# First convolution of images 2 to 7 on 64x32 tiles of TensorE, with a DMA-made copy for the shifted corner

## Chip, cores, metric

One Trainium2 chip, one of its cores. The metric is the device time of one execution in microseconds (us). A time below is counted from the start of the profiled execution's span unless it is a duration.

## What is computed

The input x is 8 images of 32 channels, 128 x 128, float32. Cut to what matters, the reference is:

```
def _gn(v):        # groups of 2 channels, mean and variance over a group and the whole image
    ...
def _L0_conv_ref(x, weight, bias):     # x and weight quantised with one scale per tensor
    s = max(|x|);  q = clip(round(x * 127 / s), -127, 127)
    out = conv3x3(qx, qw, padding=1) * (sx * sw / 127**2) + bias
def _L1_conv_ref(image, weight1, weight2):
    kern = einsum(weight, PSI)                       # 3x3 kernels
    h = leaky(instnorm(conv3x3(image, kern1)))
    return leaky(instnorm(conv3x3(h, kern2)))
x = x + _L0_conv_ref(_gn(x), weight, bias)           # "x1" below
x = x + _L1_conv_ref(_gn(x), weight1, weight2)
```

So each image passes three 3x3 convolutions of 32 to 32 channels. Here they are called conv0 (quantised, fp16 operands), conv1 and conv2 (float32).

## The kernel before

**Layout.** An image of 128 x 128 is cut by the parity of column and row into four planes of 64 x 64, and the 128 partitions hold (column parity px, row parity py, channel). So a plane has 32 partitions, and partitions 0 to 63 are the even columns, 64 to 127 the odd ones. `xs` holds all 8 images. A tile with a border of zeros (66 x 66) feeds a convolution: `qpad` (fp16, the quantised image) conv0, `apad` conv1, `hpad` conv2.

**Tiles of TensorE.** A 3x3 tap of a full-size image becomes a tap among the four planes. The weights are gathered into 32-column blocks by how far the window is shifted: `own` (none), `side` (one column), `vert` (one row), `corn` (both). conv0 reads all 128 partitions for each plane of the output: a tile is 128 rows by 32 columns, 4 of them stand side by side, and each half unit (one PSUM bank, 512 columns) needs 4 parts of 4 matmuls. conv1 and conv2 work with 64x32 tiles, 8 side by side: 4 matmuls read 64 partitions for bank `hp` and 4 the other 64 partitions for the other bank; after that the halves change places. They need no corner: the missing taps are inside the 64 partitions.

**Units.** An image is 4 units of 2 PSUM banks. The results go through `ring`, 3 slots of 2 banks. A unit's first matmul waits until the unit 3 places before it was taken out of PSUM (`wait_slot`). conv0's units are taken by VectorE (`x1_unit`: times `dequant`, plus x, into `xs`), those of conv1 and conv2 by ScalarE (`take`), after VectorE's statistics of them (`conv_stats`).

**Order.** Every engine's order is written out by hand. After a head (loading, group statistics, the global maximum, images 0 and 1 of conv0) come six periods t = 0 to 5, and TensorE does in each conv1 of image t, conv0 of image t + 2 and conv2 of image t. Small 128x128 matmuls (`gather`) sum the statistics over partitions. The chain between conv1 and conv2 is: statistics of conv1's last unit, `spread_conv`, gather ("c1"), `group_moments` on VectorE, `norm_c` on GpSimd, four pieces `make_h` on ScalarE, conv2. GpSimd quantises image t + 3 during period t, in four pieces of three instructions (`quantise`) through the scratch tile `scaled`. SyncE issues all DMAs: the loads, and in the periods the stores of finished images, each behind a wait for its data.

Of the kernel before, what the change touches and what calls it, by code (L numbers as in the profile page):

```python
# [15 lines left out]
P = 128  # L16
# [67 lines left out]
def conv_block_kernel(nc, x_d, w0_d, bias_d, w12_d, const_d, out_d):  # L84
    psi = disco_psi()
    with ExitStack() as ctx:
# [12 lines left out]
        scaled = [sb(f"scaled{p}", [P, QCOLS], F32) for p in range(2)]  # L99
# [8 lines left out]
        corn0 = sb("corn0", [P, 2, 2, C], F16)  # L108
        own12 = sb("own12", [P, 2, 2, 2, C], F32)
# [3 lines left out]
        bias = sb("bias", [P, 1], F32)  # L113
        minus_half = sb("minus_half", [P, 1], F32)
        wmax = sb("wmax", [P, 1], F32)
        wmax_all = sb("wmax_all", [P, 1], F32)
        wmul = sb("wmul", [P, 1], F32)
        amax = sb("amax", [P, B + 1], F32)
        amax1 = sb("amax1", [P, 1], F32)
        sx = sb("sx", [P, 1], F32)  # L120
        sx_inv = sb("sx_inv", [P, 1], F32)
        qmul = sb("qmul", [P, 1], F32)
        dequant = sb("dequant", [P, 1], F32)
# [6 lines left out]
        bn = {s: sb(f"bn_{s}", [P, BANKS, 6], F32) for s in STAGES}  # L130
# [9 lines left out]
        kern = sb("kern", [P, 2 * TAPS * C], F32)[0:C].rearrange("p (v k o) -> p v k o", v=2, k=TAPS)  # L140
        kern0 = sb("kern0", [P, TAPS * C], F16)[0:C].rearrange("p (k o) -> p k o", o=C)
        centre = sb("centre", [P, 1], F32)
        var_eps = {s: sb(f"var_eps_{s}", [P, 1], F32) for s in STAGES[1:]}
        scale = {s: sb(f"scale_{s}", [P, 2], F32) for s in STAGES[1:]}
        shift = {s: sb(f"shift_{s}", [P, 2], F32) for s in STAGES[1:]}
# [66 lines left out]
        out_ready = sem("out_ready")  # L212
        q_one_scaled = sem("q_one_scaled")
# [63 lines left out]
        def _(sp):  # L277
# [8 lines left out]
            for b in range(1, B):  # L286
                if b >= 2:

                    sp.wait_ge(x_in[b - 2], 16)
                if b == B - 1:  # L290
                    sp.wait_ge(kern_done, 1)
                    sp.wait_ge(kern0_done, 1)
                load(b)
            for t in range(B):
                parts = 4 if t == B - 1 else 2
                for n in range(parts):
# [3 lines left out]
                                 xs_cols(t, n * cols, cols)).then_inc(stored_first if t < 4 else stored, 16)  # L300
            sp.wait_ge(stored_first, 16 * 8)
# [3 lines left out]
        def _(act):  # L305
            def assemble(kernel, own, side, vert, corn):
# [3 lines left out]
                for qx in range(2):  # L310
                    for qy in range(2):
# [7 lines left out]
                        if corn is not None:  # L319
                            last = nc.scalar.copy(corn[q, 1 - qx, 1 - qy, :], k[:, 1 - dx, 1 - dy, :])  # L320
# [30 lines left out]
            assemble(kern0, own0, side0, vert0, corn0).then_inc(weights0_ready, 1)  # L351
# [6 lines left out]
            def affine0(n):  # L358
# [3 lines left out]
                if n >= 2:  # L362
                    act.wait_ge(q_ready, n - 1)
                nc.scalar.activation(scaled[n % 2][:, 0:(r1 - r0) * BLK], xs_rows(0, r0, r1), ACT.Identity,  # L364
                                     bias=q_shift[:, 0:1], scale=q_scale[:, 0:1]).then_inc(q_scaled, 1)

            def affine_one(n):


                r0, r1 = EDGES[n:n + 2]  # L370
                nc.scalar.activation(flat(hpad)[:, r0 * BLK:r1 * BLK], xs_rows(1, r0, r1), ACT.Identity,
# [116 lines left out]
            assemble(kern[:, 0], own12[:, 0], side12[:, 0], vert12[:, 0], None)  # L488
            assemble(kern[:, 1], own12[:, 1], side12[:, 1], vert12[:, 1], None).then_inc(weights12_ready, 1)
# [7 lines left out]
        def _(pool):  # L497
# [116 lines left out]
            def quantise(b, n):  # L614
                r0, r1 = EDGES[n:n + 2]
                rows = scaled[n % 2][:, 0:(r1 - r0) * BLK]
                at = 4 * (b - 2) + n
                pool.wait_ge(q_ready, 4 * (b - 1) + max(n - 1, 0))
# [21 lines left out]
            norm_x1(0)  # L640
            quant_pieces(2, 0)
# [27 lines left out]
        def _(dve):  # L669
            nc.vector.memset(qpad[:, 0, :], 0.0)  # L670
            nc.vector.memset(qpad[:, PAD - 1, :], 0.0)
            nc.vector.memset(qpad[:, 1:PAD - 1, 0:1], 0.0)
            nc.vector.memset(qpad[:, 1:PAD - 1, PAD - 1:PAD], 0.0)
            for tile in (own0, side0, vert0, corn0, own12, side12, vert12):
# [431 lines left out]
```

## Time and profile before

| | |
|---|---|
| median of 3 runs | 389.82 us (389.71 to 390.39) |
| the profiled execution | 390.26 us |
| its span, first to last instruction | 388.4 us |
| mean granted TensorE clock | 0.984 of full |
| one period (t = 2) | 185.21 to 221.64 |

A timeline row gives start and duration in us, engine (PE = TensorE, PEld = its weight loads, DVE = VectorE, ACT = ScalarE, POOL = GpSimd, SP = SyncE), the line of the kernel, the operation, output and inputs, their shapes and how many instructions are merged; in brackets the idle time before and what ended it. A float32 matmul leaves two records.

### The profile page before, as it was taken

What the parts mean: (1) busy time and instruction counts of PE and PEld (TensorE: products, weight loads), DVE (VectorE), ACT (ScalarE), POOL (GpSimd) and SP (SyncE); (2) the same over time, 40 slices, a digit from 0 to 9 for tenths busy, and PEclk for the clock granted to TensorE, in tenths of its full rate; (3) what the DMA queues carried; (4) which work ended last, traced back from release to release, by engine and by line L of the source; (5) the groups of instructions that cost most, each with busy time, mean ns of one, the idle gap of its engine ahead of it and who ended that gap; (6) DMA issues with size and microseconds to landing.
All of it is one profiled execution on the core that took longest, in us unless ns stands there. A gap on an engine that the chain in (4) does not pass through costs nothing.

```text
span 388.4 us, 11585 instructions
## 1 busy us (share of the span) xinstructions
PE 301.1 (78%) x5224; PEld 118.5 (31%) x5224; DVE 279.4 (72%) x418; ACT 234.4 (60%) x243; POOL 159.4 (41%) x248
## 2 busy tenths in 40 slices
PE   0000100397999999999999999999999999999950
PEld 0000100353233334333433343333334333333310
DVE  3828899789869559857974995699559846543485
ACT  1089996295334574477527753764565579766554
POOL 0189887247928441562438063607451011101100
PEclk9999999999899999999999999999999999999995
DMA  7999500000000005001400220040005000400055
GB/s 275 396 429 432 246 1 1 0 2 2 3 2 2 3 2 219 3 2 41 180 2 3 110 111 3 3 201 21 2 2 219 2 2 30 192 3 2 2 218 216
DMA packets 4176, 34.77 MB, mean 90 GB/s; under 512 B 608, under 2 KB 768, under 8 KB 1280
## 3 DMA queue, kind: packets, MB, share of 16 engines
q1 hardware_dynamic: 4128, 34.04, 21.5%
q8 instruction: 41, 0.67, 0.7%
q14 instruction: 7, 0.06, 0.1%
HBM read 17.26 MB, written 16.78 MB: 88 GB/s over the span
## 4 chain that ended last, share of the span: by engine, by line
PE 57%; DVE 27%; POOL 7%; issue 3%; DMA 2%; ACT 2%; SPq 0%; DVEq 0%; POOLq 0%
PE ring L964 43%; PE ring L1024 8%; DVE amax L745 8%; DVE xs L827 7%; DVE bn_c L810 6%; PE ring L970 3%; DMA xs<-w_dram 2%; POOL apad L571 2%; DVE xs L794 2%; PE gathered_in L928 1%; DVE bn_x L800 1%; DVE bn_x L723 1%; ACT scaled L364 1%; POOL xs L510 1%; PE gathered_gn L928 1%
## 5 line engine op out<-in xcount | busy, mean ns | idle before, releaser
L810 DVE BATCH_NORM_STATS2 bn_c<-ring 128x6 f32<-128x512 f32 x128 | 82.7, 688 | 61.7 <-PE ring L970 61.7
L970 PE MATMUL ring<-apad,own 64*32 64x512 f32 x448 | 59.2, 597 | 0.0
L381 ACT COPY apad<-ring 128x1024 f32<-128x1024 f32 x28 | 28.4, 1013 | 50.9 <-DVE bn_c L810 50.2
L964 PE MATMUL ring<-apad,own 64*32 64x512 f32 x448 | 59.0, 597 | 0.0
L964 PE MATMUL ring<-hpad,own 64*32 64x512 f32 x448 | 58.7, 592 | 0.0
L970 PE MATMUL ring<-hpad,own 64*32 64x512 f32 x448 | 58.5, 592 | 0.0
L964 PE MATMUL ring<-hpad,vert 64*32 64x512 f32 x448 | 58.3, 587 | 0.0
L970 PE MATMUL ring<-apad,side 64*32 64x512 f32 x448 | 58.2, 587 | 0.0
L970 PE MATMUL ring<-hpad,side 64*32 64x512 f32 x448 | 58.0, 587 | 0.0
L964 PE MATMUL ring<-apad,vert 64*32 64x512 f32 x448 | 57.9, 587 | 0.0
L539 POOL TENSOR_SCALAR var_eps_c<-moments_c 128x1 f32<-128x1 f32 x16 | 3.0, 190 | 127.0 <-DVE moments_c L718 126.6
L381 ACT COPY hpad<-ring 128x1024 f32<-128x1024 f32 x28 | 28.3, 1012 | 26.0 <-DVE bn_c L810 25.5
L413 ACT ACTIVATE apad<-apad,shift_c,scale_c 128x1024 f32<-128x1024 f32 x28 | 34.1, 1242 | 14.6 <-POOL shift_c L551 14.6
L794 DVE SCALAR_TENSOR_TENSOR xs<-ring,dequant,xs 128x1024 f32<-128x1024 f32 x32 | 39.9, 1275 | 2.4 <-PE ring L1024 2.4
L404 ACT ACTIVATE hpad<-hpad,shift_c,scale_c 128x1024 f32<-128x1024 f32 (+2 forms) x28 | 32.8, 1235 | 14.6 <-POOL shift_c L551 14.6
L800 DVE BATCH_NORM_STATS2 bn_x<-xs 128x6 f32<-128x512 f32 x64 | 39.4, 679 | 0.0
L827 DVE SCALAR_TENSOR_TENSOR xs<-apad,bias,xs 128x1024 f32<-128x1024 f32 x28 | 35.1, 1273 | 1.8 <-ACT apad L413 1.8
L394 ACT ACTIVATE apad<-xs,shift_x,scale_x 128x1024 f32<-128x1024 f32 (+2 forms) x28 | 33.2, 1237 | 4.7 <-POOL shift_x L548 4.7
L745 DVE TENSOR_REDUCE amax<-apad 128x1 f32<-128x4096 f32 (+1 forms) x7 | 26.3, 3788 | 8.1 <-POOL apad L571 8.1
L619 POOL TENSOR_SCALAR scaled<-xs,q_scale,q_shift 128x1024 f32<-128x1024 f32 (+2 forms) x24 | 28.7, 1196 | 0.0
L331 ACT ACTIVATE qpad<-xs 128x4096 f16<-128x4096 f32 x5 | 18.0, 3608 | 16.6 <-DMA xs<-x_dram 16.6
L1043 PE MATMUL gathered_gn<-spread_x,const 128*128 128x24 f32 x6 | 1.8, 388 | 32.6 <-DVE spread_x L731 32.6
(139 smaller groups left out, 620.8 us busy)
## 6 DMA issues: line engine op xcount, KB each, us to landing
xs<-x_dram SPq DMA_DIRECT2D x8, 2048.0 KB, 10.2
out_dram<-xs SPq DMA_DIRECT2D x14, 1024.0 KB, 4.3
out_dram<-xs SPq DMA_DIRECT2D x4, 512.0 KB, 2.9
xs<-w_dram SPq DMA_DIRECT2D x1, 288.0 KB, 8.9
const<-const_dram SPq DMA_DIRECT2D x1, 146.0 KB, 2.4
xs<-w_dram SPq DMA_DIRECT2D x1, 36.0 KB, 1.8
bias<-bias_dram SPq DMA_DIRECT2D x1, 0.5 KB, 2.4
```

The source lines that it names most:

```text
L381: nc.scalar.copy(unit_of(tile, u), grid(slot(v, t, u))).then_inc(taken[v], 1)
L394: nc.scalar.activation(rows_of(a_tile(b), r0, r1), grid(xs_rows(b, r0, r1)), ACT.Identity, bias=param(shift["x1"], b), scale=param(scale[" ...
L404: nc.scalar.activation(rows, rows, ACT.Prelu, bias=param(shift["c1"], t), scale=param(scale["c1"], t), alpha=SLOPE).then_inc(h_ready, 1)
L413: nc.scalar.activation(rows, rows, ACT.Prelu, bias=param(shift["c2"], t), scale=param(scale["c2"], t), alpha=SLOPE).then_inc(out_norm, 1)
L745: nc.vector.tensor_reduce(amax[:, n:n + 1], gn_tile(b)[:, c0:c1], AX.X, ALU.max, apply_absolute_value=True).then_inc(max_done, 1)
L794: nc.vector.scalar_tensor_tensor(x, slot(0, b, u), dequant[:], x, ALU.mult, ALU.add).then_inc(taken[0], 1)
L800: ins = nc.vector.bn_stats(bn["x1"][:, k, :], xs_cols(b, k * BANK, BANK))
L810: ins = nc.vector.bn_stats(bn[s][:, u * UBANKS + h, :], ring_of(v, t, u)[:, h, :])
L827: nc.vector.scalar_tensor_tensor(x, unit_of(a_tile(t), u), bias[:], x, ALU.add, ALU.add).then_inc(out_ready, 1)
L964: nc.tensor.matmul(bank_out(t, u, v, hp, C * (2 * px + py), C), wv[q0:q0 + 64, v - 1, px, py, :], window(tile, u * UBANKS + hp, dy, 0, q0, ...
L970: ins = nc.tensor.matmul(bank_out(t, u, v, hx, C * (2 * px + py), C), ws[q0:q0 + 64, v - 1, px, py, :], window(tile, u * UBANKS + hx, 0, d ...
L1024: ins = nc.tensor.matmul(bank_out(b, u, 0, h, C * (2 * px + py), C), w[:, px, py, :], window(tile, u * UBANKS + h, dy, dx), start=part == ...
```

## The change

conv0 of images 2 to 7 (of images 0 and 1 not) is written like conv1 and conv2, in half units on 64x32 tiles (`taps0`, `first0`, `second0`, `conv0`). A half has three parts, own, vert and side, for the one half of the tiles, and own, vert and a shifted corner for the other. That corner's source lies in the other 64 partitions, so it reads `qturn`, a copy of `qpad` with the two halves of the partitions exchanged, and the weights `turn0`. SyncE makes the copy with two DMAs of 64 partitions (`turn`), once an image is fully quantised. The gathers stand behind `second0(b, 0)`. VectorE takes the moments of conv1 ahead of x1's first unit. To make room for `qturn`, one of the two `scaled` tiles goes (its remaining one also holds `kern` and `kern0` in the head, small tiles are merged), `affine0` writes to `hpad` without waiting, and `quantise` waits for the piece before it.

```
-        scaled = [sb(f"scaled{p}", [P, QCOLS], F32) for p in range(2)]
+        qturn = sb("qturn", [P, PAD, PAD], F16)
+        scaled = sb("scaled", [P, QCOLS], F32)
...
+            def turn(b):
+                if b > 2:
+                    sp.wait_ge(conv_done[0], UNITS * b)
+                sp.wait_ge(q_ready, 4 * b)
+                for half in range(2):
+                    to, at = 64 * half, 64 * (1 - half)
+                    sp.dma_start(qturn[to:to + 64, 1:1 + BLK, :], qpad[at:at + 64, 1:1 + BLK, :]).then_inc(q_turned, 16)
+            turn(2)
+            turn(3)
             for t in range(B):
...
+                if t + 4 < B:
+                    turn(t + 4)
...
                         if corn is not None:
-                            last = nc.scalar.copy(corn[q, 1 - qx, 1 - qy, :], k[:, 1 - dx, 1 - dy, :])
+                            nc.scalar.copy(corn[q, 1 - qx, 1 - qy, :], k[:, 1 - dx, 1 - dy, :])
+                            last = nc.scalar.copy(turned[q, qx, 1 - qy, :], k[:, 1 + dx, 1 - dy, :])
...
-                if n >= 2:
-                    act.wait_ge(q_ready, n - 1)
...
-                pool.wait_ge(q_ready, 4 * (b - 1) + max(n - 1, 0))
+                pool.wait_ge(q_ready, 4 * (b - 1) + n)
...
             norm_x1(0)
+            pool.wait_ge(weights12_ready, 1)
             quant_pieces(2, 0)
...
+                group_moments("c1", t)
                 x1_unit(t + 2, 0)
-                group_moments("c1", t)
                 x1_unit(t + 2, 1)
...
+            def taps0(b, u, hp, start, stop):
+                hx = 1 - hp
+                for n in range(3):
+                    for px in range(2):
+                        for py in range(2):
+                            q0, dy = 64 * px, 1 if py else -1
+                            tile, w, dy, dx = ((qpad, own0, 0, 0), (qpad, vert0, dy, 0),
+                                               (qturn, turn0, dy, 1 if px else -1))[n]
+                            nc.tensor.matmul(bank_out(b, u, 0, hp, C * (2 * px + py), C), w[q0:q0 + 64, px, py, :],
+                                             window(tile, u * UBANKS + hp, dy, dx, q0, 64),
+                                             start=start and n == 0, stop=stop and n == 2)
+                    for px in range(2):
+                        for py in range(2):
+                            q0, dx, dy = 64 * (1 - px), 1 if px else -1, 1 if py else -1
+                            w, dy, dx = ((own0, 0, 0), (vert0, dy, 0), (side0, 0, dx))[n]
+                            ins = nc.tensor.matmul(bank_out(b, u, 0, hx, C * (2 * px + py), C), w[q0:q0 + 64, px, py, :],
+                                                   window(qpad, u * UBANKS + hx, dy, dx, q0, 64),
+                                                   start=start and n == 0, stop=stop and n == 2)
+                return ins
+            def first0(b, u):
+                wait_slot(0, b, u)
+                pe.wait_ge(q_turned, 32 * (b - 1))
+                taps0(b, u, 0, True, False).then_inc(crossed0, 1)
+            def second0(b, u):
+                pe.wait_ge(crossed0, UNITS * (b - 2) + u + 1)
+                taps0(b, u, 1, False, True).then_inc(conv_done[0], 1)
+            def conv0(b, gathers):
+                first0(b, 0)
+                first0(b, 1)
+                second0(b, 0)
+                for g in gathers:
+                    gather(*g)
+                first0(b, 2)
+                second0(b, 1)
+                second0(b, 2)
+                first0(b, 3)
+                second0(b, 3)
```

TensorE's instructions for one unit of conv0 of a later image, before (`32x512` is the output: 32 partitions, 512 columns; this is half a unit, the other half repeats it without the wait):

```order
L1024 MATMUL ring<-qpad,own0 32x512 [waits q_ready,conv1_taken]
L1024 MATMUL ring<-qpad,own0 32x512 x3
L1024 MATMUL ring<-qpad,side0 32x512 x4
L1024 MATMUL ring<-qpad,vert0 32x512 x4
L1024 MATMUL ring<-qpad,corn0 32x512 x4
```

and after (`first0`; `second0` is the same with a wait for `crossed0`):

```order
L1057 MATMUL ring<-qpad,own0 32x512 [waits q_turned,conv1_taken]
L1057 MATMUL ring<-qpad,own0 32x512 x3
L1064 MATMUL ring<-qpad,own0 32x512 x4
L1057 MATMUL ring<-qpad,vert0 32x512 x4
L1064 MATMUL ring<-qpad,vert0 32x512 x4
L1057 MATMUL ring<-qturn,turn0 32x512 x4
L1064 MATMUL ring<-qpad,side0 32x512 x4
```

A unit has 32 matmuls before and 48 after, an image 128 and 192; the first matmul waits for the copy in place of the quantised piece.

VectorE's rows behind the statistics of conv1's last unit, in a period with t >= 1, before:

```order
L817 BN_AGGR own_stat_c<-bn_c 128x2 [waits conv1_counted]
L819 TENSOR_TENSOR spread_c<-const,own_stat_c 128x12 [waits stat_step_c1]
L794 SCALAR_TENSOR_TENSOR xs<-ring,dequant,xs 128x1024 [waits conv0_done]
L718 BN_AGGR moments_c<-gathered_in 128x2 [waits gathered_c1]
L794 SCALAR_TENSOR_TENSOR xs<-ring,dequant,xs 128x1024 [waits conv0_done]
L800 BN_STATS bn_x<-xs 128x6 [waits x1_done]
```

and after (`single` holds `dequant` now):

```order
L832 BN_AGGR own_stat_c<-bn_c 128x2 [waits conv1_counted]
L834 TENSOR_TENSOR spread_c<-const,own_stat_c 128x12 [waits stat_step_c1]
L733 BN_AGGR moments_c<-gathered_in 128x2 [waits gathered_c1]
L809 SCALAR_TENSOR_TENSOR xs<-ring,single,xs 128x1024 [waits conv0_done] x2
L815 BN_STATS bn_x<-xs 128x6 [waits x1_done]
```

The wait for the gather now stands right behind the instruction that the gather itself waits for, and x1's units stand behind both.

SyncE's queue behind the loads, after (before, only the stores stood there):

```order
L301 DMA qturn<-qpad 64x4224 [waits q_ready]
L301 DMA qturn<-qpad 64x4224
L301 DMA qturn<-qpad 64x4224 [waits q_ready,conv0_done]
L301 DMA qturn<-qpad 64x4224
L310 DMA out_dram<-xs 128x2048 [waits out_ready] x2
L301 DMA qturn<-qpad 64x4224 [waits q_ready,conv0_done]
```

Each copy is two DMAs of 64 partitions x 4224 fp16 values (528 KB); from image 4 on it stands behind the stores of image t - 4.

## Rows read from the trace of the kernel before

**Rows 1.** Windows: busy us of PE, PEld, DVE, ACT, POOL; granted clock; DMA.

```profile
185.21:221.64 36.43, 36.31 (x654) 13.82 (x646) 27.41 (x44) 21.74 (x20) 16.31 (x22) 1.00 0.15 60
```

**Rows 2.** Timeline of TensorE, conv0 of image 4 and conv2 of image 2.

```profile
185.37 0.41 PE L1024 MATMUL ring<-qpad,own 128*32 128x512 f16 x4
...
188.31 0.39 PE L928 MATMUL gathered_in<-spread_c,const 128*128 128x12 f32 x2
188.63 0.41 PE L1024 MATMUL ring<-qpad,own 128*32 128x512 f16 x4
...
192.81 0.40 PE L1024 MATMUL ring<-qpad,corn 128*32 128x512 f16 x4
193.14 0.63 PE L964 MATMUL ring<-hpad,own 64*32 64x512 f32 x4
...
200.18 0.40 PE L928 MATMUL gathered_gn<-spread_x,const 128*128 128x24 f32 x2
...
202.25 0.61 PE L964 MATMUL ring<-hpad,own 64*32 64x512 f32 x4
```

**Rows 3.** Timeline of VectorE in the same stretch.

```profile
188.09 0.17 DVE L819 TENSOR_TENSOR spread_c<-const,own_stat_c 128x12 f32<-128x12 f32 x1
...
189.37 0.20 DVE L718 BATCH_NORM_AGGREGATE moments_c<-gathered_in 128x2 f32<-128x12 f32 x1
189.75 1.28 DVE L794 SCALAR_TENSOR_TENSOR xs<-ring,dequant,xs 128x1024 f32<-128x1024 f32 x1 [0.18 <-PE ring L1024]
...
198.85 0.18 DVE L709 TENSOR_TENSOR spread_x<-const,own_stat_x 128x24 f32<-128x24 f32 x1
198.95 1.29 DVE L810 BATCH_NORM_STATS2 bn_c<-ring 128x6 f32<-128x512 f32 x2
```

**Rows 4.** Timeline of ScalarE in the same stretch.

```profile
187.68 1.01 ACT L381 COPY hpad<-ring 128x1024 f32<-128x1024 f32 x1 [1.37 <-DVE bn_c L810]
190.89 4.65 ACT L404 ACTIVATE hpad<-hpad,shift_c,scale_c 128x1088 f32<-128x1088 f32 x4 [2.20 <-POOL shift_c L551]
200.28 1.01 ACT L381 COPY apad<-ring 128x1024 f32<-128x1024 f32 x1 [4.73 <-DVE bn_c L810]
```

**Rows 5.** TensorE's sequencer, line 979 (`first_half`), 200 to 200.7 us.

```profile
L979 PEldq EVENT_SEMAPHORE  x1: 51/51/51, 200.6 to 200.6; - x1
```

**Rows 6.** DMA issues: KB each, median us from issue to landing.

```profile
xs<-x_dram SPq DMA_DIRECT2D x8, 2048.0 KB, 10.2
out_dram<-xs SPq DMA_DIRECT2D x14, 1024.0 KB, 4.3
out_dram<-xs SPq DMA_DIRECT2D x4, 512.0 KB, 2.9
```

**Rows 7.** Timelines in period t = 0: GpSimd, then TensorE, then VectorE.

```profile
108.47 1.00 POOL L627 TENSOR_SCALAR qpad<-scaled 128x960 f16<-128x960 f32 x1
...
112.27 0.41 PE L1024 MATMUL ring<-qpad,own 128*32 128x512 f16 x4
...
127.65 0.63 PE L964 MATMUL ring<-hpad,own 64*32 64x512 f32 x4
...
116.90 1.28 DVE L794 SCALAR_TENSOR_TENSOR xs<-ring,dequant,xs 128x1024 f32<-128x1024 f32 x1 [0.79 <-PE ring L1024]
...
126.11 1.29 DVE L810 BATCH_NORM_STATS2 bn_c<-ring 128x6 f32<-128x512 f32 x2
```

**Rows 8.** Timeline of GpSimd, the last piece of an image's quantising, period t = 2.

```profile
210.19 0.99 POOL L622 TENSOR_SCALAR scaled<-scaled 128x960 f32<-128x960 f32 x1
211.27 1.00 POOL L627 TENSOR_SCALAR qpad<-scaled 128x960 f16<-128x960 f32 x1
```

**Rows 9.** Windows around TensorE's idle time in the head.

```profile
91.70:94.90 3.20, 0.45 (x10) 0.32 (x8) 2.60 (x7) 0.00 (x0) 1.53 (x7) 1.00 0.00 0
94.90:97.60 2.70, 2.70 (x32) 0.92 (x32) 2.31 (x2) 2.30 (x2) 2.46 (x4) 0.65 0.00 0
97.60:99.50 1.90, 1.90 (x28) 0.58 (x32) 1.69 (x2) 1.90 (x3) 1.74 (x3) 0.60 0.03 9
```

More of the change, by code:

```diff
@@ L112, in conv_block_kernel @@
         const = sb("const", [P, 2 * P + 3 * (GN_MEMBERS + IN_MEMBERS)], F32)
[L113 to L117, printed above, removed]
-        amax = sb("amax", [P, B + 1], F32)
[L119 to L123, printed above, removed]
+        single = sb("single", [P, 11], F32)
+        bias, minus_half, wmax, wmax_all, wmul, amax1, sx, sx_inv, qmul, dequant, centre = (
+            single[:, n:n + 1] for n in range(11))
+        amax = sb("amax", [P, B + 1], F32)
         gn_scale = sb("gn_scale", [P, B], F32)
@@ L129, in conv_block_kernel @@
         STAGES = ("x", "x1", "c1", "c2")
-        bn = {s: sb(f"bn_{s}", [P, BANKS, 6], F32) for s in STAGES}
+        bn = {s: sb(f"bn_{s}", [P, BANKS, 6], F32) for s in STAGES[1:]}
+        bn["x"] = bn["c2"]
         own_stat = {s: sb(f"own_stat_{s}", [P, 3], F32) for s in STAGES[1:]}
@@ L139, in conv_block_kernel @@
         var_eps_x = sb("var_eps_all", [P, B], F32)
[L140 to L145, printed above, removed]
+        kern = scaled[0:C, 0:2 * TAPS * C].rearrange("p (v k o) -> p v k o", v=2, k=TAPS)
+        kern0 = scaled[0:C, 2 * TAPS * C:].bitcast(F16)[:, 0:TAPS * C].rearrange("p (k o) -> p k o", o=C)
+        var_eps_tile = sb("var_eps", [P, 3], F32)
+        var_eps = {s: var_eps_tile[:, n:n + 1] for n, s in enumerate(STAGES[1:])}
+        params = sb("params", [P, 2, 6], F32)
+        scale = {s: params[:, 0, 2 * n:2 * n + 2] for n, s in enumerate(STAGES[1:])}
+        shift = {s: params[:, 1, 2 * n:2 * n + 2] for n, s in enumerate(STAGES[1:])}
         stage_at = (B - 1) * COLS
@@ L305, in _, with assemble @@
         def _(act):
-            def assemble(kernel, own, side, vert, corn):
+            def assemble(kernel, own, side, vert, corn, turned):
                 k = kernel.rearrange("p (ty tx) o -> p tx ty o", ty=3)
@@ L669, in _ @@
         def _(dve):
-            nc.vector.memset(qpad[:, 0, :], 0.0)
-            nc.vector.memset(qpad[:, PAD - 1, :], 0.0)
+            for tile in (qpad, qturn):
+                nc.vector.memset(tile[:, 0, :], 0.0)
+                nc.vector.memset(tile[:, PAD - 1, :], 0.0)
             nc.vector.memset(qpad[:, 1:PAD - 1, 0:1], 0.0)
             nc.vector.memset(qpad[:, 1:PAD - 1, PAD - 1:PAD], 0.0)
-            for tile in (own0, side0, vert0, corn0, own12, side12, vert12):
+            for tile in (own0, side0, vert0, corn0, turn0, own12, side12, vert12):
                 nc.vector.memset(tile[:], 0.0)
```

21 lines of the change are left out of this document (11 added, 10 removed).

## Prediction, made before the changed kernel ran

> **What bounds the kernel now.** I read the windows of one period first: TensorE is busy in 36.31 of 36.43 us, VectorE in 27.41 [rows 1]. Six such periods make more than half of the span, so TensorE's time in a period seems to be the whole story. The timelines of the three engines around conv0 correct that. TensorE starts conv0 of an image at 185.37, is at the gather of conv1's statistics at 188.31, goes on at 188.63 and starts conv2 at 193.14 [rows 2]. The gather does not start when the matmuls ahead of it are through: its input is ready at 188.09 + 0.17 = 188.26, and it starts 0.05 later [rows 2, 3]. That 0.05 is my figure for a semaphore below. So the middle of conv0 is already paced by VectorE. VectorE then works through four `x1_unit`, eight statistics and three small instructions with one pause of 0.18, until it comes to conv2's first unit at 198.95 [rows 3]. By the order of the code TensorE has to wait for two things here: the gather of x1 (200.18) needs `spread_x` (198.85 + 0.18 = 199.03), and conv2's `first_half` 3 (202.25) needs the slot of unit 0, which ScalarE empties from 200.28 to 201.29 [rows 2 to 4]. Both are there about 1.0 us ahead of TensorE. That 1.0 is what a shorter conv0 can give before VectorE takes over.
>
> **The change: pace of the new matmuls.** Before, 4 matmuls start each (192.81 - 188.63) / 19 = 0.22 us, 0.055 each [rows 2]. 128 of them take 7.04 us. The new 192 stand 8 side by side: with 0.22 for 8 they take 24 x 0.22 = 5.28, 1.76 less for an image. That the array can do 8 at a time is shown by conv2 (64*32 in its rows), at float32 though; no row shows it at fp16. An upper bound is the pace that rows do show for one matmul, 0.055: 192 x 0.055 = 10.6 us. What speaks for the lower end: the sequencer must hand out twice as many instructions in the same time, and after the gather of 200.18 the sequencer's event of the next `first_half` is at 200.6 [rows 2, 5]. Between them by program order stand the gather and a half of 32 matmul records, each with its weight load, some 68 instructions in 0.42 us, 6 ns each, if the sequencer stood at the gather's wait. Eight matmuls with their loads are 16 instructions, so 0.10 us of 0.22. I take 0.22, and keep 0.27 (17 ns each) as a middle case and 0.43 as the bad end. The Trainium skill, "TensorE: Matmul & The Clock Gate", section "Wait — 56ns, not 53.3ns?", gives a floor of about 25 ns from matmul to matmul, and about 62 ns where firmware decodes them. By the first an image would take 4.8 us and nothing changes; by the second 11.9 us. The rows above, at 55 ns, are already below 62, so this case's trace speaks against the second.
>
> **One period, step by step** (the times of rows 2 to 4, conv0 again from 185.37). The first three halves are 9 groups, 1.98 us, with a short wait in front of the second for ScalarE's take of conv1's unit 2; they are through well ahead of 188.26. So the gather stays at 188.31: **this half of the saving is worth nothing.** It ends 188.70. VectorE now waits for it, and takes the moments at 188.75 instead of 189.37; the chain to conv2's input (GpSimd, then ScalarE from 190.89, first piece 1.3) comes 0.62 earlier, 191.57. The first x1 unit moves from 188.18 to about 188.95. `first0` 2 needs the slot that ScalarE empties at 187.68 + 1.01 = 188.69 [rows 4], so it starts at 188.75. Two halves later, 188.75 + 5 x 0.22 + 0.40 + 0.05 = 190.30, unit 1 of x1 can be taken; before it was taken at 189.75 [rows 3]. From here VectorE's row is as before without a gap, **0.55 later**. Five halves from 188.75 are 3.30, so conv2 starts at about 192.1, 1.0 earlier than 193.14, and its input is there. But VectorE comes to conv2's unit 0 at 198.95 + 0.55 = 199.50. The gather of x1 can start at 199.03 + 0.55 + 0.05 = 199.63 (0.55 earlier), and ScalarE's take ends at 201.29 + 0.55 = 201.84, so `first_half` 3 starts at 201.9 instead of 202.25. From there to the next conv0 the rows repeat: **0.35 us less per period**, of the 1.76 saved on TensorE. With 0.27 per group: unit 1 is taken 0.25 later, and 0.1 per period is left.
>
> **The first copy.** Image 2 is fully quantised at 108.47 + 1.00 = 109.47, and its conv0 starts at 112.27 [rows 7], 2.8 us later. The copy is 2 x 528 KB. Its price stands in no row; the nearest are stores of 512 KB, 2.9 us, and of 1024 KB, 4.3 [rows 6]; from both sides: 2.9 if the two run wholly beside each other, 10.2 (2048 KB) as the far end. Both go to one queue at once, so I take 4.3 for the two: there at 113.8, and TensorE waits some 1.6 us. Then 9 groups and two gathers (0.3 apart, the next matmul 0.32 behind): the rest goes on at 116.5, x1's unit 1 is taken at 116.5 + 1.1 + 0.45 = 118.05 instead of 116.90 [rows 7], VectorE reaches conv2's unit 0 at 126.11 + 1.15 = 127.26, the slot is free 1.29 + 0.04 + 1.01 later (199.50 to 201.84), 129.6, and TensorE takes it at 129.65; before, it was there at 127.65 + 1.75 = 129.4. So period 0 **loses 0.3**. If the copy takes 2.9, period 0 gains: x1's unit 1 is taken about 0.2 earlier than before, and since VectorE was 1.1 ahead of TensorE in this period, up to 1.1 is won.
>
> **The rest.** Twelve DMAs more on SyncE's queue. `turn(t + 4)` stands behind store t and ahead of store t + 1, which comes only in the next period, so no store is held up. In the later periods the last piece is quantised at 211.27 + 1.00 = 212.27 [rows 8] and conv0 starts at 185.37 + 36.43 = 221.80 [rows 1, 2]: 9.5 us of cover for a copy of 4.3; without that cover it would cost what period 0 pays. Four small copies on ScalarE and three memsets on VectorE lie in idle time of the head, ahead of the maximum that everything waits for there. `affine0` loses a wait behind the maximum, but what comes out of that ends at the copy's wait. GpSimd's new wait for the weights has them done: ScalarE, which writes them, is ahead by its order of the work that GpSimd's step just before releases. `quantise` waits for its predecessor on its own engine; such a wait costs 211.27 - 210.19 - 0.99 = 0.09 [rows 8], once in each pair of pieces. Behind it in GpSimd's queue is `norm_c` for conv2, which conv1 of the next image needs late; I count 0.1 once, for period 4, where GpSimd also clears two borders.
>
> **Sum**, against the profiled execution of 390.26 (span 388.4 and 1.9 around it), 0.44 above the median: +0.3 + 0.1 - 5 x 0.35 = -1.35. Median: 389.82 - 1.35 = 388.5. A change under 0.2%, 0.78 us, can't be told from none.
>
> **Rivals.**
> - *VectorE does not bind* (0.15): x1's units slip into gaps, or the copy is there in time. TensorE then keeps up to 1.0 per period: 389.8 - 3 to -6, 384 to 387. For it: 1.0 of slack in rows 2 to 4. Against it: VectorE has one gap of 0.18 in 10 us, and the new order puts a wait of 0.44 into it.
> - *Feeding binds at 17 ns an instruction* (0.13): 0.1 per period, period 0 some 0.5 lost: 389.8. For it: every stretch of rows shows 27 ns or more as a lasting pace, only a burst shows 6.
> - *The first copy is late, and the clock falls* (0.14). The trace has this once: TensorE was busy for 0.45 of the 3.20 us to 94.90, and then had the lower level (1.2 GHz) for part of the next 4.6, granted 0.65 and 0.60: 2.70 x 0.35 + 1.90 x 0.40 = 1.7 us lost [rows 9]. Here the idle time would be 1.6, half as long. With it: 388.5 + 1.7 = 390.2. Each us of the copy beyond 4.3 adds one more; from 6.4 on alone, or 5 with the clock, it is slower than before, 391.
> - *Feeding binds at the pace shown, 0.43 for 8* (0.08). Unit 1 of x1 comes 1.05 later than in my case, conv2 starts at 188.75 + 15 x 0.43 = 195.2, 2.1 later than before: 6 x 2.1 = 12 us, 402. The limit is at 0.28 us for 8, from where VectorE's row eats the gain.
> - My forecast has the other 0.50.
>
> **From these to the numbers.** Half of the forecast's weight and the first rival are faster, with a little of the forecast's on this side of 0.2%: faster 0.58, same 0.22, slower 0.20. The range leaves out the last rival and the far part of the first: 385.8 to 391.3.
>
> **What will show it.** Groups of 8 matmuls 0.22 us apart in conv0, the c1 gather still waiting for `spread_c`, the moments 0.6 earlier, x1's unit 1 about 2.0 behind the gather, VectorE without a pause up to conv2's unit 0; TensorE with new waits ahead of x1's gather and `first_half` 3; periods of 36.1; the first copy landing 4.3 us behind its issue and a wait of 1.6 at 112. Wrong would make it: other distances between the groups, or a copy of another length.

## The result, and the profile after

The changed kernel takes **394.2 us** (393.76 to 395.33, 4 runs) beside 390.11 (389.71 to 390.89, 4 runs) for the one before: ratio 1.012, 95% interval 1.009 to 1.015. It is slower; I had forecast 388.5 and a faster kernel, with 391.3 as the upper end. The profiled executions took 393.76 and 390.26 us, their spans are 392.0 and 388.4.

The first place to look is where image 2's conv0 starts. Timeline of TensorE in period 0 of the changed kernel:

```profile
110.01 0.59 PE L985 MATMUL ring<-apad,side 64*32 64x512 f32 x4
116.77 0.61 PE L1057 MATMUL ring<-qpad,own 64*32 64x512 f16 x4 [6.16 <-DMA qturn<-qpad]
...
117.15 0.66 PE L1057 MATMUL ring<-qpad,vert 64*32 64x512 f16 x4
...
117.58 0.66 PE L1057 MATMUL ring<-qturn,turn 64*32 64x512 f16 x4
...
120.14 0.44 PE L1057 MATMUL ring<-qturn,turn 64*32 64x512 f16 x4
...
120.52 0.40 PE L943 MATMUL gathered_gn<-spread_x,const 128*128 128x24 f32 x2
```

TensorE stands for 6.16 us until the copy has landed, and then nine of its groups of eight matmuls start 0.42 us apart on average (116.77 to 120.14 are eight distances) instead of 0.22. The windows of the same kernel show both; the first four are 1 us long (columns: window and its length, PE, PEld, DVE, ACT, POOL busy with counts, granted clock, DMA share, GB/s):

```profile
109.60:110.60 1.00, 1.00 (x24) 0.09 (x8) 0.67 (x2) 0.29 (x1) 0.01 (x1) 1.00 0.00 0
110.60:111.60 1.00, 0.00 (x2) 0.00 (x0) 0.91 (x2) 0.72 (x1) 0.00 (x0) 1.00 1.19 253
...
112.60:113.60 1.00, 0.00 (x0) 0.00 (x0) 0.00 (x1) 0.44 (x1) 0.00 (x0) 0.90 1.04 220
113.60:114.60 1.00, 0.00 (x0) 0.00 (x0) 0.00 (x0) 0.00 (x0) 0.00 (x0) 0.50 1.05 262
...
110.60:115.60 5.00, 0.00 (x2) 0.00 (x0) 1.84 (x4) 1.74 (x2) 0.00 (x0) 0.78 0.96 216
...
117.00:121.00 4.00, 4.00 (x76) 1.80 (x60) 0.04 (x1) 0.00 (x0) 0.00 (x0) 0.60 0.02 4
```

The last quantised piece is there at 109.60; DMA engines are busy from 110.6 to 115.6 and move 216 GB/s. From 113.6 on the granted clock is 0.50: the lower of TensorE's two levels, 1.2 GHz, after a stretch without any matmul. It stays there while the nine groups run; the 0.60 of the last window is a mean of that and of the full clock behind them.

Now the periods. The window of t = 2 in the changed kernel, to be read against [rows 1]:

```profile
189.83:225.97 36.14, 35.05 (x718) 12.94 (x710) 27.40 (x44) 21.79 (x20) 16.39 (x22) 1.00 0.29 91
```

36.14 us instead of 36.42 from one conv0 to the next, and TensorE is busy in only 35.05 of it. The timelines of TensorE, VectorE and ScalarE there answer to [rows 2 to 4]:

```profile
189.83 0.39 PE L1057 MATMUL ring<-qpad,own 64*32 64x512 f16 x4
190.05 0.40 PE L1057 MATMUL ring<-qpad,vert 64*32 64x512 f16 x4
...
190.98 0.40 PE L1057 MATMUL ring<-qpad,own 64*32 64x512 f16 x4 [0.28 <-ACT hpad L394]
...
192.93 0.39 PE L943 MATMUL gathered_in<-spread_c,const 128*128 128x12 f32 x2 [0.43 <-DVE spread_c L834]
193.37 0.41 PE L1057 MATMUL ring<-qpad,own 64*32 64x512 f16 x4
...
196.97 0.60 PE L979 MATMUL ring<-hpad,own 64*32 64x512 f32 x4
...
204.30 0.40 PE L943 MATMUL gathered_gn<-spread_x,const 128*128 128x24 f32 x2 [0.24 <-DVE spread_x L724]
```

```profile
192.70 0.17 DVE L834 TENSOR_TENSOR spread_c<-const,own_stat_c 128x12 f32<-128x12 f32 x1
193.36 0.21 DVE L733 BATCH_NORM_AGGREGATE moments_c<-gathered_in 128x2 f32<-128x12 f32 x1 [0.48 <-PE gathered_in L943]
...
194.96 1.28 DVE L809 SCALAR_TENSOR_TENSOR xs<-ring,single,xs 128x1024 f32<-128x1024 f32 x1 [0.24 <-PE ring L1064]
...
204.06 0.18 DVE L724 TENSOR_TENSOR spread_x<-const,own_stat_x 128x24 f32<-128x24 f32 x1
204.16 1.29 DVE L825 BATCH_NORM_STATS2 bn_c<-ring 128x6 f32<-128x512 f32 x2
206.69 1.29 DVE L825 BATCH_NORM_STATS2 bn_c<-ring 128x6 f32<-128x512 f32 x2 [1.24 <-PE ring L985]
```

```profile
194.89 4.65 ACT L417 ACTIVATE hpad<-hpad,params 128x1088 f32<-128x1088 f32 x4 [1.58 <-POOL params L564]
```

TensorE now has waits at both gathers, each for VectorE. The chain that ended last turns from one engine to the other; its shares by engine, of the changed kernel:

```profile
DVE 40%; PE 37%; POOL 11%; DMA 4%; issue 3%; ACT 3%; SPq 1%; DVEq 0%; POOLq 0%
```

In the kernel before, the page has PE at 57% and DVE at 27% of that chain.

One trap in comparing the two profiles lies in the head. The kernel before was profiled with the clock at 0.65 and 0.60 there [rows 9]; over 95 to 100 us it is 0.66 in one and 1.00 in the other, before and then changed:

```profile
95.00:100.00 5.00, 5.00 (x64) 1.53 (x65) 4.41 (x5) 4.65 (x4) 4.68 (x5) 0.66 0.01 3
```

```profile
95.00:100.00 5.00, 5.00 (x96) 1.97 (x96) 5.00 (x7) 4.65 (x4) 4.65 (x5) 1.00 0.01 3
```

The runs below show this fall in some profiles and not in others, with nearly the same code in the head. GpSimd, which sets the moment of the copy, does not follow TensorE's clock: from the x1 gather in the head to the last quantised piece it takes 16.76 us in the changed kernel (92.84 to 109.60) and 16.77 in the run "clock kept" below (93.87 to 110.64), whose profile has the fall. So in the changed kernel the fall should change only how long TensorE waits; one of its four executions, without a trace, had a mean granted clock of 0.967 instead of 0.976 and took 395.33, which this does not explain.

### The profile page after: what moved, and what is told of

It reads as the page before. It is cut to its first block, busy times and chain, and to the rows that moved or that the text cites. A ratio compares the mean times of both kernels' runs of the same rounds, so it can differ in the third digit from the quotient of the medians.

```text
span 392.0 us, 12378 instructions
## 1 busy us (share of the span) xinstructions
PE 293.6 (75%) x5608; PEld 116.4 (30%) x5608; DVE 280.0 (71%) x421; ACT 235.0 (60%) x247; POOL 160.0 (41%) x248
## 4 chain that ended last, share of the span: by engine, by line
DVE 40%; PE 37%; POOL 11%; DMA 4%; issue 3%; ACT 3%; SPq 1%; DVEq 0%; POOLq 0%
PE ring L979 29%; DVE bn_x L815 9%; DVE amax L760 8%; DVE xs L809 7%; DVE xs L842 7%; DVE bn_c L825 6%; PE ring L1057 3%; PE ring L985 2%; DMA xs<-w_dram 2%; POOL apad L584 2%; POOL scaled L632 2%; DMA qturn<-qpad 2%; POOL scaled L635 2%; POOL qpad L640 2%; DVE bn_c L738 1%
## 5 line engine op out<-in xcount | busy, mean ns | idle before, releaser
L985 PE MATMUL ring<-apad,own 64*32 64x512 f32 x448 | 58.5, 591 | 0.0
L979 PE MATMUL ring<-apad,own 64*32 64x512 f32 x448 | 58.4, 591 | 0.0
L552 POOL TENSOR_SCALAR var_eps<-moments_c 128x1 f32<-128x1 f32 x16 | 3.1, 192 | 129.6 <-DVE moments_c L733 129.2
L417 ACT ACTIVATE hpad<-hpad,params 128x1024 f32<-128x1024 f32 (+2 forms) x28 | 32.7, 1234 | 18.6 <-POOL params L564 18.6
L426 ACT ACTIVATE apad<-apad,params 128x1024 f32<-128x1024 f32 x28 | 34.1, 1241 | 14.3 <-POOL params L564 14.3
L809 DVE SCALAR_TENSOR_TENSOR xs<-ring,single,xs 128x1024 f32<-128x1024 f32 x32 | 39.5, 1264 | 1.3 <-PE ring L1064 1.2
L842 DVE SCALAR_TENSOR_TENSOR xs<-apad,single,xs 128x1024 f32<-128x1024 f32 x28 | 35.1, 1273 | 1.5 <-ACT apad L426 1.0
L407 ACT ACTIVATE apad<-xs,params 128x1024 f32<-128x1024 f32 (+2 forms) x28 | 33.2, 1238 | 4.7 <-POOL params L561 4.7
L640 POOL TENSOR_SCALAR qpad<-scaled 128x1024 f16<-128x1024 f32 (+2 forms) x24 | 25.2, 1051 | 2.5 <-POOL scaled L635 1.0
```

Source lines behind the costliest of these rows:

```text
L407: nc.scalar.activation(rows_of(a_tile(b), r0, r1), grid(xs_rows(b, r0, r1)), ACT.Identity, bias=param(shift["x1"], b), scale=param(scale[" ...
L426: nc.scalar.activation(rows, rows, ACT.Prelu, bias=param(shift["c2"], t), scale=param(scale["c2"], t), alpha=SLOPE).then_inc(out_norm, 1)
L640: nc.gpsimd.tensor_scalar(rows_of(qpad, r0, r1), grid(rows), 1.0, -ROUND, ALU.mult, ALU.add).then_inc(q_ready, 1)
L809: nc.vector.scalar_tensor_tensor(x, slot(0, b, u), dequant[:], x, ALU.mult, ALU.add).then_inc(taken[0], 1)
L842: nc.vector.scalar_tensor_tensor(x, unit_of(a_tile(t), u), bias[:], x, ALU.add, ALU.add).then_inc(out_ready, 1)
L979: nc.tensor.matmul(bank_out(t, u, v, hp, C * (2 * px + py), C), wv[q0:q0 + 64, v - 1, px, py, :], window(tile, u * UBANKS + hp, dy, 0, q0, ...
```

## Experiments

Starts and periods are TensorE's, from the traces. "Period" is the one of t = 2. Ratios are against the kernel before, run beside them (its medians there: 390.38, 390.51 and 389.37 us, and 389.33 in the one run beside the two queues). The starts of image 2 also hold what happens ahead of it: the x1 gather in the head came anywhere from 92.51 to 93.87 us in these profiles.

| kernel | median us | ratio, 95% interval | image 2 starts | period | clock 95 to 100 |
|---|---|---|---|---|---|
| before | 390.11 | 1 | 112.27 | 36.42 | 0.66 |
| changed | 394.20 | 1.012 (1.009 to 1.015) | 116.77 | 36.14 | 1.00 |
| image 2 whole | 387.83 | 0.994 (0.992 to 0.996) | 111.09 | 36.14 | 1.00 |
| split copy | 387.21 | 0.992 (0.989 to 0.995) | 112.91 | 36.13 | 0.66 |
| clock kept | 393.16 | 1.008 (1.005 to 1.011) | 119.41 | 36.14 | 0.66 |
| straight copy | 391.73 (one run) | | 114.83 | 36.14 | 1.00 |
| two straight copies | 394.69 (one run) | | 117.55 | 36.13 | 1.00 |
| two queues | 394.22 (one run) | | 117.03 | 36.14 | 1.00 |
| split copy, moments back | 387.74 | 0.993 (0.991 to 0.995) | 111.79 | 36.13 | 0.66 |
| split copy, output late | 383.45 | 0.983 (0.981 to 0.986) | 111.14 | 35.51 | 1.00 |
| + unit 1 first | 383.23 | 0.982 (0.980 to 0.985) | 112.07 | 35.30 | 0.66 |
| + filled | 381.59 | 0.980 (0.977 to 0.983) | 110.01 | 35.31 | 1.00 |
| before, moments first | 389.50 | 1.000 (0.998 to 1.002) | 111.92 | 36.42 | 0.74 |
| before, output late | 389.14 | 0.999 (0.996 to 1.001) | 110.19 | 36.23 | 1.00 |
| before, filled | 388.99 | 0.999 (0.997 to 1.000) | 111.12 | 36.43 | 1.00 |

**Is the first copy the loss?** Image 2 in the old form:

```diff
-            turn(2)
...
-                conv0(t + 2, [("x1", 1), ("c1", t)] if t == 0 else [("c1", t)])
+                if t == 0:
+                    conv0_pair(2, 0, gather_after=("x1", 1))
+                    conv0_pair(2, 1, gather_after=("c1", 0))
+                    conv0_pair(2, 2)
+                    conv0_pair(2, 3)
+                else:
+                    conv0(t + 2, [("c1", t)])
```

> The changed kernel, but the first convolution of image 2 in its old whole-tile form, with no copy to wait for; images 3 to 7 as changed. Theory (late copy: TensorE stood 6.2 us for the two copies of image 2 and then ran 9 groups at 0.43 instead of 0.22 us): image 2 starts within 0.5 us of 110 instead of at 116.77, needs the old 8.0 us up to the second convolution's start (118.2 instead of 124.66), so 6.4 us less: 387.8 us, 0.994 of the kernel before. Periods 1 to 5 stay 0.28 us shorter each than before. Rival (the loss sits in the 64-row form or in every copy, and period 0 only shows it first): at most 1.8 us come back, 392.4 or more. Side question: the kernel before had its clock at 0.66 from 95 to 100 us and the changed one at 1.00; if that was chance and the dip returns, 1.8 us more, 389.6.

387.83 us: the theory's number, 6.4 us below the changed kernel, with the later periods unchanged at 36.14. Image 2 starts at 111.09, outside the half us named around 110; the x1 gather in this profile is itself 0.57 later (93.41 against 92.84). Its first convolution takes the old 8.0 us. So the loss is image 2's, and the rest of the change is a gain.

**The same with the copy cut up:**

```diff
-            turn(2)
+            for n in range(4):
+                r0, r1 = EDGES[n:n + 2]
+                sp.wait_ge(q_ready, 4 + n + 1)
+                for half in range(2):
+                    to, at = 64 * half, 64 * (1 - half)
+                    sp.dma_start(qturn[to:to + 64, 1 + r0:1 + r1, :], qpad[at:at + 64, 1 + r0:1 + r1, :]
+                                 ).then_inc(turned2[n], 16)
...
+                if b == 2:
+                    pe.wait_ge(turned2[u], 32)
...
```

> The changed kernel, but the copy of image 2 cut into the four pieces in which it is quantised, each issued when its piece is there (4 x 2 DMAs of about 132 KB, with a semaphore per piece), and TensorE waits for the piece that it needs. Theory (only the last piece's wait and a short transfer remain): the copies of pieces 0 to 2 land before 109, that of piece 3 by 112.5, where TensorE comes to unit 3 only at about 114; image 2 starts near 110.2, its convolution takes 7.1 us as in later periods, the second convolution starts at 117.3 instead of 124.66: 7.3 us less, 386.9 us (0.992 of before). Rival (a copy costs mostly a fixed time and eight in a row on one queue add up): the last lands past 115 and TensorE waits at unit 3, 389 to 391. Rival (loss is elsewhere): 393 or more.

387.21, 0.3 above the theory. DMA issues of this kernel, 95 to 125 us, and its TensorE:

```profile
qturn<-qpad SPq DMA_DIRECT2D x4, 132.0 KB, 2.6
qturn<-qpad SPq DMA_DIRECT2D x2, 140.2 KB, 2.7
qturn<-qpad SPq DMA_DIRECT2D x2, 123.8 KB, 2.3
```

```profile
112.91 0.39 PE L1064 MATMUL ring<-qpad,own 64*32 64x512 f16 x2
...
115.36 0.40 PE L950 MATMUL gathered_gn<-spread_x,const 128*128 128x24 f32 x2
...
119.50 0.60 PE L986 MATMUL ring<-hpad,own 64*32 64x512 f32 x4
```

No wait for a copy is left, the pitch is 0.22 from the first group on, and conv2 starts 6.6 us behind conv0. It starts later than I expected (119.50, not 117.3) for two reasons: the x1 gather in the head is 0.93 later than in the changed kernel's profile (93.77 against 92.84), and this profile has the fall of the clock behind it.

**Is the slow pitch the clock?**

```diff
                 wait_slot(0, b, u)
+                if b == 2 and u == 0:
+                    keep_clock(110, 0)
```

> The changed kernel with 110 matmuls of 128 columns (results thrown away) in front of image 2's first convolution, while the copies are under way; the wait for them stays. Theory (the clock fell because TensorE stood still): start of image 2 unchanged at 116.8, but its first 9 groups at 0.22 instead of 0.43 us: 1.9 us less, 392.3 us. Rival (the low pitch of these groups is the first use of the copied tile or of new weights): the pitch stays 0.43 and the time 394.2.

```profile
113.16 6.32 PE L950 MATMUL ring<-side,own 128*128 128x128 f16 x110
119.41 0.40 PE L1057 MATMUL ring<-qpad,own 64*32 64x512 f16 x4
...
119.64 0.39 PE L1057 MATMUL ring<-qpad,vert 64*32 64x512 f16 x4
```

The pitch is 0.23 and 0.22 from the start, at a granted clock of 1.00, so the 0.43 was the clock, as the theory has it. What the clock cost is less than the 1.9 that I had expected: from image 2's first matmul to the matmul behind the two gathers it is 4.29 us in the changed kernel (116.77 to 121.06) and 2.65 here (119.41 to 122.06), 1.6 less. The time fell by 1.0: conv1(0) ended later in this profile, at 113.1 (the head up to the x1 gather was 1.03 later, and the fall came on top), and the 110 matmuls then ran to 119.4. The copy, issued at 110.66, would by the 7.1 us of the changed kernel have let TensorE go on at 117.8, so in such an execution the filling is some 1.6 us too long, by this estimate.

**Why did the copy take 7 us?** One DMA over 128 rows, then two of 64 rows that don't exchange, then the exchange from two queues:

```diff
-                for half in range(2):
-                    to, at = 64 * half, 64 * (1 - half)
-                    sp.dma_start(qturn[to:to + 64, 1:1 + BLK, :], qpad[at:at + 64, 1:1 + BLK, :]).then_inc(q_turned, 16)
+                sp.dma_start(qturn[:, 1:1 + BLK, :], qpad[:, 1:1 + BLK, :]).then_inc(q_turned, 16)
...
```

> The changed kernel with one DMA from 128 rows to the same 128 rows (1,056 KB) in place of two that exchange the halves of 64 rows; the shifted corner is then computed from unexchanged rows, so that term of the output is another one. Theory A (a copy within on-chip memory of 1 MB just takes about 6.5 us, half the rate of a store to DRAM): landing 6 to 7 us after the issue, total within 0.5 us of 394.2. Theory B (64 rows reach only part of the engines or memory ports, so the exchange is what costs): landing after 4.3 us as a 1,024 KB store, image 2 starts near 114.3, total about 391.7.

```diff
-                    to, at = 64 * half, 64 * (1 - half)
+                    to, at = 64 * half, 64 * half
```

> The changed kernel with its two copies of 64 rows each, but not exchanged: rows 0 to 63 to rows 0 to 63, and 64 to 127 likewise (the shifted corner is then computed from unexchanged rows). Theory A (64 rows per DMA cost the rate): as the exchange, transfers active 4.9 us, landing after 6.2 to 7, image 2 starts at 116.8. Theory B (crossing between the halves of the memory costs it): as the single straight copy, 2.8 us active, landing after 5.1, start at 114.8, time 391.7.

```diff
-                for half in range(2):
+                for half in range(1 if b == 2 else 2):
...
+                if t == 0:
+                    act.wait_ge(q_ready, 8)
+                    act.dma_start(qturn[64:128, 1:1 + BLK, :], qpad[0:64, 1:1 + BLK, :]).then_inc(q_turned, 16)
```

> The changed kernel, but the second of image 2's two copies is issued from ScalarE's queue at the moment at which SyncE issues the first. Theory A (each 64-row transfer is limited by itself, in one queue they go one after the other): side by side both need half the time, transfers active for about 2.8 us as for the single copy of 128 rows, image 2 starts near 114.8 instead of 116.8, about 391.7 us in all. Theory B (the 16 engines are shared and slow for 64 rows whatever the queue): active 5 us, start at 116.8 or later, 394.2.

Windows over the transfers of the three kernels (straight, two straight, two queues), each followed by its own DMA issues (KB each, median us to landing):

```profile
110.80:113.80 3.00, 0.00 (x0) 0.00 (x0) 1.72 (x4) 1.53 (x2) 0.00 (x0) 1.00 0.95 346
```

```profile
qturn<-qpad SPq DMA_DIRECT2D x1, 1056.0 KB, 5.1
```

```profile
111.20:116.20 5.00, 0.07 (x8) 0.00 (x0) 1.84 (x4) 1.80 (x2) 0.00 (x0) 0.84 0.97 211
```

```profile
qturn<-qpad SPq DMA_DIRECT2D x2, 528.0 KB, 5.6
```

```profile
110.60:115.60 5.00, 0.30 (x8) 0.00 (x0) 1.84 (x4) 2.03 (x2) 0.00 (x0) 0.86 0.93 208
```

```profile
qturn<-qpad SPq DMA_DIRECT2D x1, 528.0 KB, 4.5
qturn<-qpad ACTq DMA_DIRECT2D x1, 528.0 KB, 7.0
```

Over 128 rows 346 GB/s and about 3 us of transfer; in two DMAs over 64 rows 211, and 216 with the exchange. From the end of GpSimd's last piece to image 2's first matmul it is 5.23 us with the straight copy, 7.32 with two straight copies, 7.15 with two queues and 7.17 in the changed kernel. So crossing the halves costs nothing, and 64 rows a DMA cost some 2 us. The straight copy differs from the two in the number of DMAs too, and no run here splits a copy over 128 rows; but the number alone hardly halves the rate, since the loads of 2048 KB over 128 rows, several in a row on one queue, ran at 421 GB/s (window 10 to 40 us of the kernel before). The single copy landed after 5.1, not the 4.3 that Theory B named, and image 2 started at 114.83, half a us later than it said; the time, 391.73, is the one it named. Two queues bring nothing, as Theory B of that run has it: issued at the same 109.91, they moved 208 GB/s together, one landed after 4.5 and the other after 7.0. Why two copies over different halves don't run at twice the rate of one, these runs leave open.

Even the straight copy leaves the kernel above the one before (391.73 in its one execution, against 388.61 to 391.34): TensorE stands for 4.2 us, and the granted clock is 0.53 over the next 3.5 us. The other two kernels have one execution each as well.

**What sets the period?** First the moments back behind x1's unit 0, in the kernel with the split copy:

```diff
-                group_moments("c1", t)
                 x1_unit(t + 2, 0)
+                group_moments("c1", t)
                 x1_unit(t + 2, 1)
```

> The kernel with the split copy (387.2 us), with the c1 moments behind x1's unit 0 again, as in the kernel before. Theory (in the changed kernel VectorE's unit 1 waits for TensorE's second half of unit 1, 0.24 us in a period, so the moments' place costs the x1 chain nothing, and TensorE has 0.41 us to spare at the x1 gather): h's input 0.75 us later, the second convolution starts up to 0.4 us later, the x1 gather where it was; no change, within 0.3% of 387.2. Rival (the moments in front are what gives the 0.28 us a period): 0.3 us a period come back, 388.7. Second rival (TensorE's start of the second convolution carries through to the end): 0.5 us a period, 389.7.

387.74 beside 387.21 is no difference that these runs can tell from none, and the period is the same, 36.13; conv2 starts 7.13 us behind conv0 as before the move, not up to 0.4 later. Its VectorE timeline shows why: unit 1 waits for TensorE, 5.12 us behind the start of conv0 (184.12), where it is 5.13 with the moments in front.

```profile
187.08 1.28 DVE L816 SCALAR_TENSOR_TENSOR xs<-ring,single,xs 128x1024 f32<-128x1024 f32 x1
188.27 0.20 DVE L740 BATCH_NORM_AGGREGATE moments_c<-gathered_in 128x2 f32<-128x12 f32 x1
189.24 1.28 DVE L816 SCALAR_TENSOR_TENSOR xs<-ring,single,xs 128x1024 f32<-128x1024 f32 x1 [0.77 <-PE ring L1071]
```

The same move in the kernel before:

> The kernel before, with nothing changed but the c1 moments in front of x1's unit 0. Theory (TensorE sets the period of the kernel before: it is busy 36.3 of 36.4 us and reaches the x1 gather 1.2 us after its input is there): x1's chain starts 0.45 us later, which that 1.2 us hides, h's input is 0.6 us earlier and nothing waits for it: 390.4 us, no change. Rival (VectorE's chain sets the period of the kernel before too): 0.45 us a period later, 393.0.

Ratio 1.000 and 36.42 a period, as in the kernel before: the theory holds. Then VectorE's last output of image t-1 moved out of the way of conv1's statistics, in the kernel with the split copy and in the kernel before:

```diff
                 conv_stats(1, t, 2)
-                if before:
-                    output(t - 1, 3)
                 conv_stats(1, t, 3)
...
                 conv_stats(2, t, 0)
+                if before:
+                    output(t - 1, 3)
                 conv_stats(2, t, 1)
```

> The kernel with the split copy, with VectorE's output of the last unit of image t-1 (1.27 us, in front of conv1's last statistics) moved to behind the first statistics of the second convolution, where VectorE waits 1.24 us for TensorE. Theory (in periods 1 to 5 VectorE's chain from the end of conv1 to the x1 gather sets the time, not TensorE, which is busy 35.05 of 36.14 us): the statistics end 0.85 us earlier, the c1 gather comes when TensorE reaches it (2.5 us after the start of the first convolution instead of 3.10), unit 1 of x1 0.43 earlier, the x1 gather too: 0.43 us a period, 385.0 us. Rival (TensorE's own work sets the period): no change, 387.2. Rival (the late output delays a buffer or a store): above 388.

> The kernel before, with nothing changed but VectorE's last output of image t-1 behind the first statistics of the second convolution. Theory (TensorE sets the period of the kernel before, the late output pays only once the first convolution is shorter): 36.4 us a period as before, at most 0.1 less, 390.0. Rival (VectorE's chain binds there too): 0.6 us a period, as in the changed kernel, 387.

One window of a period each, first with the split copy, then of before:

```profile
182.24:217.75 35.51, 34.91 (x718) 12.93 (x710) 27.46 (x43) 21.86 (x20) 16.33 (x22) 1.00 0.29 93
```

```profile
183.08:219.31 36.23, 36.23 (x655) 13.82 (x647) 27.53 (x42) 21.74 (x21) 16.31 (x22) 1.00 0.15 59
```

In the kernel with the split copy the one move is worth 0.62 us a period (theory 0.43; 383.45 instead of 385.0), 3.1 in five periods. The medians are 3.8 apart; four of the five executions with the split copy had a mean granted clock of 0.981 or 0.982, and four of the five with the late output 0.986 or 0.987, so the rest is probably the fall in the head, of which more below. In the kernel before the move is worth 0.19, somewhat above the 0.1 that the theory allowed and far below the rival's 0.6; the medians can't tell it from none, and TensorE is then busy without a gap. It comes at the c1 gather, which stands 2.75 us behind the start of conv0 (185.83 - 183.08) instead of 2.94. So the kernel before was bound by TensorE but for these 0.2, and the changed one by VectorE. Last, the order in conv0:

```diff
-                first0(b, 2)
                 second0(b, 1)
-                second0(b, 2)
+                first0(b, 2)
                 first0(b, 3)
+                second0(b, 2)
                 second0(b, 3)
```

> The kernel with the split copy and the late output, and in the first convolution the second half of unit 1 directly behind the gather, then the first halves of units 2 and 3, then the second halves of units 2 and 3. Theory (with the statistics earlier, unit 1 is what VectorE waits for next, and TensorE waits 0.26 us for the first half of unit 3 to drain in front of its second): unit 1 is there 0.66 us earlier, VectorE takes it 0.3 us earlier, the x1 gather likewise: 0.3 us a period less than with the late output alone, 383.5 us. Rival (TensorE binds once the output is late): only the 0.26 us drain comes back or nothing, 384 to 385.

The period falls by 0.21 to 35.30, two thirds of what was expected; the medians, 383.23 and 383.45, do not separate the two kernels.

**The fall in the head.**

```diff
             conv0_pair(1, 2)
+            fill(16)
             gather("x1", 0)
+            fill(22)
             conv0_pair(1, 3)
```

`fill(n)` is n matmuls of 128 columns into the bank of the c1 gather, which nobody reads then.

> The kernel before, with 16 matmuls of 128 columns (results thrown away) in front of the first x1 gather and 22 behind it, where TensorE waits 1.3 and 1.5 us for VectorE at 91.7 to 94.9 us. Theory (the clock at 95 to 100 us falls in some executions, 0.66 in the profile of the kernel before and of two of its variants, 1.00 in others, because of these waits, and this is also what spreads one kernel's times over 2 us): the clock stays at 1.00 in the profile, conv1(0) starts 1.8 us earlier than with the fall, the median falls by 1 to 1.8 us, 388.8 to 389.4, and the spread of the times shrinks below 1.5 us. Rival (the fall has another cause): 390.4, spread as before.

> The kernel with the split copy, the late output and unit 1 first (383.2 us), with the same two fillings in front of and behind the first x1 gather. Theory (as for the kernel before): no clock at 0.66 in 95 to 100 us, median 1 to 1.8 us less, 381.4 to 382.2. Rival: 383.2.

Neither profile has the fall. The kernel before then takes 388.3 to 390.09 us in 12 runs, unfilled 387.99 to 391.43 in 29 beside it: the longest times are gone, but the spread of 1.8 is above the 1.5 named, and the median moves by less than the runs resolve.

The mean granted clock of each execution shows why. Of the 29, 16 have 0.987 or 0.988 and a median of 389.05 us, 13 have 0.979 to 0.984 and a median of 390.43; the profiles with the fall have 0.982 to 0.984. So the fall costs this kernel some 1.4 us when it comes, it came in less than half of these executions, and the filled kernel's 388.99 is the time of those without it. (In the two other comparisons 13 of 17 and 11 of 13 executions of the kernel before are in the slower group; that is why its median there is 390.4 and 390.5.) The filling itself costs nothing that shows: the gather starts 0.06 us behind the end of `spread_x` with it (93.39, 93.45) and without it (92.93, 92.99), and the next matmul 1.89 us behind the gather in both.

With everything together it is **381.59 us**, 0.980 (0.977 to 0.983) of the kernel before, inside the theory's 381.4 to 382.2; how much of the 1.64 below the unfilled kernel is the filling, five and six overlapping executions can't tell exactly.

## Why the prediction was wrong

**The step that failed is the price of the first copy.** I took 4.3 us from a store of 1024 KB [rows 6] and had it landed at 113.8; TensorE could use it at 116.77, 2.97 later. From the last quantised piece it took 7.17 us. The store has 128 rows, each copy has 64: that is 1.9 of the miss, by the straight copy's 5.23. Another 0.9 the copy over 128 rows took beyond the store's 4.3, and 0.13 is GpSimd's last piece being later. The nearest row in bytes was not the nearest in shape. The Trainium skill has the rule, in "SBUF — State Buffer", section "Door 1: The DMA port swizzle (why `[64,N]` ≈ `[32,N]`)": rows 0 to 63 and rows 64 to 127 reach 8 of the 16 ports each, for some 218 GB/s. The trace agrees with that, with 216, 211 and 208 GB/s. The rule speaks against this change, and I had not weighed it. My own prices would have come close: each us of the copy beyond 4.3 adds one and the fallen clock 1.7, which with 2.9 us more gives 388.5 + 2.9 + 1.7 = 393.1.

**The wait of 1.6 us was 6.16.** 2.97 of the difference is the later copy. The rest is that the copy's start is fixed by GpSimd (109.60, predicted 109.47), while TensorE, without the fall in the head, was there at 110.6 instead of 112.2.

**The clock-fall rival was right in kind,** with 1.6 us (4.29 - 2.65, above) where I had 1.7. I gave it 0.14 because the idle time would be short; with a longer copy it comes along by itself.

**The sum.** Between the profiled executions I had -1.35 and found +3.50. At the conv0 of image 3 the changed kernel is 153.67 - 148.93 = 4.74 behind, where I had 0.3: 4.44 of the 4.85 is period 0. Of it 2.97 is the copy and 1.6 the clock; -0.1 is what neither explains. Periods 1 to 5, up to the first matmul of image 7's conv1 (334.44 and 331.02), brought 4.74 - (334.44 - 331.02) = 1.32 instead of 1.65: 0.33. The rest, 0.08, is behind the last period.

**The parts that held.** The pitch of the new groups is 0.22 as taken from conv2, so both rivals on feeding fall. The saving of the first halves is worth nothing, since the c1 gather waits for `spread_c` (0.43 us). VectorE takes over as the bound, and most of the 1.76 us that TensorE saves is lost to it.

**0.35 a period was 0.28.** Measured from conv0's start, the c1 gather came at 3.10 instead of 2.94, since `spread_c` itself ends 0.15 later against TensorE's start; moments, unit 1 of x1 (5.13, I had 4.93) and the x1 gather (14.47, I had 14.26) carry that on. The moments' move, which I costed as part of the gain, is worth nothing: unit 1 waits for TensorE with either order.

**The rival that VectorE does not bind** is ruled out by the late output: an edit of VectorE's order alone, with the same work, gave 0.62 us a period.

## What to carry to other kernels

Price a transfer by a row of the same shape, not only of the same bytes: two DMAs over 64 rows each ran at 0.6 of the rate of one over 128. A copy in front of the first consumer of a pipeline has no earlier work to hide behind, even where all later ones have 9 us of cover; cut it into the pieces in which its source is made. When an engine gets faster, ask which short instruction of the next one now stands in front of the result that it waits for: here one output of 1.27 us, moved into an idle gap, was worth 0.62 us a period, where the whole change was worth 0.28.

## What the runs showed of the hardware

- Within on-chip memory 1,056 KB moved at 346 GB/s over 128 rows and at 208 to 216 in two DMAs of 64 rows; crossing the halves and using a second queue changed nothing. Each figure but the 216 is from one execution of a kernel made for it.
- Matmuls of 64x32 at fp16 with 512 columns started eight every 0.22 us at the full clock and every 0.43 at the lower level, with their eight weight loads.
- With nearly the same work up to 95 us, some executions had the lower clock behind two short idle times of TensorE and others not; filling these with matmuls kept it at 1.00 in both profiles taken. The length of the first idle time does not decide it: 0.49 us went with the fall in one profile (moments back), 1.09 without it in another (changed). What does stays open.
